# Two blocks of two gated attention layers: chunk 1 of layer 0 prepared ahead of the loop, input rows loaded chunk by chunk, Newton steps of eight layer norms on VectorE

## The reference

```
x = x + tanh(g_xattn[0]) * attention0(layernorm(x), context, context, prob, mask)
x = x + tanh(g_ffn[0])   * experts0(layernorm(x))
x = x + tanh(g_xattn[1]) * attention1(layernorm(x), context, context, mask1)
x = x + tanh(g_ffn[1])   * experts1(layernorm(x))
```

## Time and profile before

| what | us |
|---|---|
| median of 3 runs | 959.44 |
| lowest, highest | 957.41, 962.17 |
| the profiled execution, its own time | 961.64 |
| its span, first to last instruction | 959.8 |
| PE (TensorE) busy | 793.3 (83%) |
| DVE (VectorE) busy | 670.6 (70%) |
| ACT (ScalarE) busy | 608.5 (63%) |
| POOL (GpSimd) busy | 571.8 (60%) |

### The profile page before, as it was taken

The page is one execution under the profiler, slowest core; times in us unless marked ns, Lnnn a source line. Parts: engine busy times, 40 slices in busy tenths (PEclk is TensorE's granted clock), DMA queues, the critical chain, the costliest instruction groups (busy, mean ns, idle before and its releaser), DMA issues.

```text
span 959.8 us, 20423 instructions
## 1 busy us (share of the span) xinstructions
PE 793.3 (83%) x6554; PEld 627.5 (65%) x6554; DVE 670.6 (70%) x1933; ACT 608.5 (63%) x2582; POOL 571.8 (60%) x872
## 2 busy tenths in 40 slices
PE   2268898988886399999876788788986889999996
PEld 1146666766664299998555556656765767888885
DVE  1246889999896534436688799998896575666664
ACT  1366888998982255444787678889996344444442
POOL 6364567888777500223477887574341767777775
PEclk9978999999996699999999889999998899999998
DMA  7929789536633742322537367454300000000000
GB/s 172 243 87 242 197 218 274 138 98 157 128 86 130 259 138 83 85 82 85 110 85 140 72 127 173 112 109 120 89 13 24 22 23 23 21 15 14 8 12 22
DMA packets 83699, 101.68 MB, mean 106 GB/s; under 512 B 8289, under 2 KB 69926, under 8 KB 82665
## 3 DMA queue, kind: packets, MB, share of 16 engines
q1 hardware_dynamic: 79496, 92.13, 37.4%
q0 software_dynamic: 4096, 8.25, 3.5%
HBM read 63.32 MB, written 45.99 MB: 114 GB/s over the span
## 4 chain that ended last, share of the span: by engine, by line
PE 41%; DVE 22%; ACT 14%; POOL 9%; issue 9%; DMA 5%; SPq 0%; POOLq 0%; ACTq 0%; DVEq 0%
ACT exp L805 10%; PE psum L654 7%; PE psum L691 5%; PE psum L693 5%; PE psum L692 5%; DVE shift L986 5%; DVE exp_T L996 2%; PE psum L542 2%; PE psum L529 2%; PE psum L642 2%; DVE ln_stats L968 2%; PE psum L643 2%; PE psum L644 2%; DVE exp_T L998 2%; PE psum L707 1%
## 5 line engine op out<-in xcount | busy, mean ns | idle before, releaser
L805 ACT ACTIVATE exp<-psum,shift 128x120 f32<-128x120 f32 x1024 | 364.8, 427 | 92.9 <-DVE shift L986 92.5
L805 ACT ACTIVATION_READ_ACCUMULATOR exp<-psum,shift 128x1 f32 x1024 | 269.8, 273 | 0.0
L986 DVE TENSOR_REDUCE shift<-psum 128x4 f32<-128x480 f32 x256 | 164.9, 646 | 55.4 <-PE psum L520 54.8
L529 PE MATMUL psum<-ident,exp 128*120 128x128 f32 x1024 | 164.5, 285 | 35.1 <-DVE exp_T L998 22.0
L1569 POOL TENSOR_TENSOR q_operand<-q_operand 128x512 f32<-128x512 f32 x96 | 125.9, 1311 | 70.3 <-DVE q_operand L1345 66.1
L1345 DVE SCALAR_TENSOR_TENSOR q_operand<-psum,comb,q_operand 128x256 f32<-128x256 f32 x256 | 111.7, 479 | 79.9 <-ACT q_operand L933 79.9
L529 PEld LDWEIGHTS psum<-ident,exp 128*120 128x120 f32 x1024 | 120.4, 143 | 53.9 <-DVE exp_T L998 26.5
L933 ACT ACTIVATE q_operand<-psum 128x512 f32<-128x512 f32 x128 | 76.4, 598 | 122.3 <-PE psum L693 122.2
L1499 POOL DMA_INDIRECT got_rows<-scratch_y,slot_get x64 | 66.9, 1046 | 121.9 <-DMA scratch_y<-y_rows 104.5
L517 PE MATMUL psum<-neg_rows,const_bf 128*128 128x480 bf16 x256 | 98.7, 386 | 48.4 <-ACT exp L805 27.5
L691 PE MATMUL psum<-w_T_high,xn_T_high 128*128 128x512 f32 x256 | 108.8, 425 | 9.5 <-DVE w_T_low L1311 7.3
(11 more groups left out here) (164 smaller groups left out, 1557.5 us busy)
## 6 DMA issues: line engine op xcount, KB each, us to landing
k_operand<-scratch_k SPq DMA_DIRECT2D x32, 360.0 KB, 6.3
q_operand<-scratch_q SPq DMA_DIRECT2D x30, 384.0 KB, 6.1
scratch_q<-parts SPq DMA_DIRECT2D x15, 384.0 KB
scratch_k<-parts SPq DMA_DIRECT2D x14, 360.0 KB, 5.2
scratch_xe<-in_zero_rows SPq DMA_DIRECT2D x8, 512.0 KB, 12.6
scratch_y<-in_zero_rows SPq DMA_DIRECT2D x8, 512.0 KB, 6.9
scratch_q<-parts SPq DMA_DIRECT2D x15, 256.0 KB
scratch_k<-parts SPq DMA_DIRECT2D x14, 240.0 KB, 5.3
```

The costliest lines, as they stand in the source:

```text
L529: ins = pe.transpose(ps[0:S2, T_BANKS[G % 2], u * S:(u + 1) * S], atts[l].expS[:, G % RING_E, u, :], ident[:, :])
L805: ins = act.activation(atts[l].expS[:, G % RING_E, u, :], ps[:, S_BANKS[G % 3], u * S2:(u + 1) * S2], ACT.Exp, bias=atts[l].shift[:, i % 2 ...
L986: dve.tensor_reduce(atts[l].shift[:, i % 2, 4 * r:4 * r + 4], ps[:, S_BANKS[G % 3], 0:4 * S2].rearrange("p (h k) -> p h k", h=4), AX_X, AL ...
```

## The change

Four things are done.

1. **READY = 2.** Chunk 1 of layer 0 is prepared ahead of the loop, behind chunk 0, on all engines; looped() leaves it out of the loop. Chunks 0 and 1 are there normalised and split by VectorE, no longer by GpSimd. SyncE fetches chunk 0's k before it stores chunk 0's q, and clears only the first q buffer before that. Chunk 2 starts at slot 2 and chunk 3 at 10.
2. **load_rows by chunk.** Rows and context of chunk 2 are loaded ahead of the loop, those of chunk c from 3 on in slot 16 c - 46, with three semaphores in turn.
3. **Newton steps.** For eight layer norms (NEWTON_ON_DVE) GpSimd stops after pow, and VectorE does three operations (roots) in the slot of the powers. VectorE's normalise_rows then subtracts the mean and multiplies by the root, so that the product of both isn't needed.
4. **Slots.** Key splits behind layer 0 move from slots 2 and 5 to 5 and 8; the gathers of layer 1's chunks 5, 6 and 7 start at slot 30, 45 and 60, not 29, 37 and 52.

```diff
+NEWTON_ON_DVE = [(0, 0), (0, 1), (0, NCH), (0, NCH + 1), (0, NCH + 2), (0, NCH + 3), (1, NCH - 2), (1, NCH - 1)]
...
+def newton_on_dve(who, n):
...
+    return (who, n) in NEWTON_ON_DVE
...
 def start_slot(l, P):
-    return ({1: 0, 2: 5, 3: 14} if l == 0 else {1: 0, 2: 0, 3: 0}).get(P, 16 * P - 38)
+    return ({1: 0, 2: 2} if l == 0 else {1: 0, 2: 0, 3: 0}).get(P, 16 * P - 38)
...
+READY = 2
...
+def looped(l, P):
...
+    return l == 1 or P >= READY
...
 def prep_at(l, P):
-    return ({1: NEAR, 2: MID} if l == 0 else {1: NEAR1, 2: MID1, 3: FAR1, 4: FAR2}).get(P, FAR)
+    return ({2: MID} if l == 0 else {1: NEAR1, 2: MID1, 3: FAR1, 4: FAR2}).get(P, FAR)
...
 def bring_slot(i):
-    return {8: 0, 9: 7, 10: 9, 11: 11}[i] if c == 2 else {3: 13, 4: 21, 5: 29, 6: 37, 7: 52}[c] + 2 * b
+    return {8: 0, 9: 7, 10: 9, 11: 11}[i] if c == 2 else {3: 13, 4: 21, 5: 30, 6: 45, 7: 60}[c] + 2 * b
...
 def add_y_slot(i):
...
-SPLIT_KEYS_AT = {2: (0, 1), 5: (2,), 19: (3, 4, 5)}
+SPLIT_KEYS_AT = {5: (0, 1), 8: (2,), 19: (3, 4, 5)}
...
-    ld_first, ld_w, ld_rows = sem("ld_first"), sem("ld_w"), sems("ld_rows", 2)
+    ld_first, ld_w, ld_rows = sem("ld_first"), sem("ld_w"), sems("ld_rows", 3)
...
-            on.wait_ge(ld_rows[min(c, 2) - 1], 32)
+            on.wait_ge(ld_rows[c % 3], 32 * ((c - 1) // 3 + 1))
...
         def attention(l):
-                project_k(0)
-                turn_rows(0, 0)
-                project_q(0)
+                for C in range(READY):
+                    project_k(C)
+                    turn_rows(0, C)
+                    project_q(C)
...
         def attention(l):
-                take_projected(1, 0)
-                part0(1, 0)
-                take_turned(0, 0)
-                make_gates()
-                take_projected(0, 0)
-                part0(0, 0)
+                for C in range(READY):
+                    take_projected(1, C)
+                    part0(1, C)
+                    take_turned(0, C)
+                    take_projected(0, C)
+                    part0(0, C)
+                    if C == 0:
+                        make_gates()
...
+        def roots(who, n, h=0):
...
+            p = CB // 2 if h else CB
+            r_s, m_v = rs[:, who, :, 0:p], mv[:, who, 0:p, :]
+            power, rstd, m = (h_pow, h_rstd, 0) if h else (ln_pow[who], ln_rstd[who], n)
+            y, t_, r, v = (r_s[:, j, :] for j in (0, 1, 2, 4))
+            on.wait_ge(power, 2 * m + 2)
+            dve.tensor_tensor(t_, y, y, ALU.mult).then_inc(rstd, 1)
+            on.wait_ge(rstd, 6 * m + 1)
+            dve.scalar_tensor_tensor(t_, v, -0.5, t_, ALU.mult, ALU.mult).then_inc(rstd, 1)
+            on.wait_ge(rstd, 6 * m + 2)
+            dve.scalar_tensor_tensor(r, t_, 1.5, y, ALU.add, ALU.mult).then_inc(rstd, 4)
...
         def normalise_rows(who, n, c, h=0):
...
-                dve.tensor_scalar(xn[:, ln_slot(who, n), b, :], x[:, c * CB + b, :], rs[:, who, 2, b:b + 1], rs[:, who, 3, b:b + 1], ALU.mult, ALU.add).then_inc(ln_norm[who], 1)
+                dve.tensor_scalar(xn[:, ln_slot(who, n), b, :], x[:, c * CB + b, :], mv[:, who, b, 0:1], rs[:, who, 2, b:b + 1], ALU.subtract, ALU.mult).then_inc(ln_norm[who], 1)
...
         def slots(n):
...
+        def split(k, C):
+            left0(k, C)
+            part1(k, C)
+            left1(k, C)
...
         def split_keys(m):
...
+                    if o == at["power"]:
+                        roots(0, C)
...
+                if l == 0 and j >= ON_DVE and o == post_at(l, j)["power"]:
+                    roots(1, j)
...
+                    roots(0, NCH)
...
+                    roots(0, HALVED, 1)
...
+        roots(0, 0)
+        normalise_rows(0, 0, 0)
+        split(1, 0)
+        stat_rows(0, 1, 0, 1)
+        split(0, 0)
+        roots(0, 1)
+        normalise_rows(0, 1, 1)
+        split(1, 1)
...
+        split(0, 1)
...
+            if newton_on_dve(who, n):
+                return
...
         def behind(l, s):
...
+        powers(0, 0)
+        pool.memset(vx[:], 0.0).then_inc(spread0, 1)
+        powers(0, 1)
...
-        pool.memset(vx[:], 0.0).then_inc(spread0, 1)
-        left0(1, 0)
-        part1(1, 0)
-        powers(0, 0)
-        left1(1, 0)
-        normalise_rows(0, 0, 0)
...
-        left0(0, 0)
-        part1(0, 0)
-        left1(0, 0)
-        add_bias(0)
+        for C in range(READY):
+            add_bias(C)
...
     def sync_program(sp):
-        def load_rows(k, c0, c1):
-            sp.dma_start(x[:, c0 * CB:c1 * CB, :], t["x"][:, c0 * CB:c1 * CB, :]).then_inc(ld_rows[k], 16)
-            sp.dma_start(ctxT[:, c0 * CK:c1 * CK], t["ctxT"][:, c0 * CK:c1 * CK]).then_inc(ld_rows[k], 16)
...
-        def clear_spares(rings):
-            for r in range(rings):
+        def load_rows(c):
+            if c > 3:
+                wait_rows(on, c - 3)
+            sp.dma_start(x[:, c * CB:(c + 1) * CB, :], t["x"][:, c * CB:(c + 1) * CB, :]).then_inc(ld_rows[c % 3], 16)
+            sp.dma_start(ctxT[:, c * CK:(c + 1) * CK], t["ctxT"][:, c * CK:(c + 1) * CK]).then_inc(ld_rows[c % 3], 16)
...
+        def clear_spares(first, end):
+            for r in range(first, end):
...
-            on.wait_ge(spare_in, 32 * (RING if C <= NCH else RING + SPOILT))
+            on.wait_ge(spare_in, 32 * (1 if C == 0 else RING if C <= NCH else RING + SPOILT))
...
-            if l == 0 and s == 0:
-                load_rows(1, 2, NCH)
+            for c in range(READY + 1, NCH):
+                if l == 0 and s == 16 * c - 46:
+                    load_rows(c)
...
-                clear_spares(SPOILT)
+                clear_spares(0, SPOILT)
...
-        load_rows(0, 1, 2)
-        clear_spares(RING)
+        clear_spares(0, 1)
+        load_rows(1)
...
+        fetch_k(0)
...
-        fetch_k(0)
...
+        load_rows(2)
+        clear_spares(1, RING)
+        for p in range(3):
+            parts_out(1, 1, p)
+        for p in range(3):
+            parts_out(0, 1, p)
+        fetch_k(1)
+        fetch_q(1)
```

More of the change, by code:

```diff
@@ L582, in behind @@
                 o, at = s - start_slot(l, P), prep_at(l, P)
+                if not looped(l, P):
+                    continue
                 if o == at["k_project"] and l == 0:
```

## The result

| | median us | lowest to highest |
|---|---|---|
| kernel before (6 runs) | 961.77 | 957.41 to 962.37 |
| changed kernel (6 runs) | 951.60 | 949.78 to 952.58 |

The ratio is 0.9906, with a 95% interval of 0.9879 to 0.9933: faster by 9.0 us on 959.4 (the two medians are 10.2 apart). The forecast was 943, a gain of 16. The range held the result, and the direction was right; the size was not. The profiled execution took 951.59, its span is 949.8 and its mean granted clock 0.943. VectorE is busy for 686.9 us where it was 670.6, GpSimd for 545.9 where it was 571.8.

What follows compares the result with a forecast made beforehand. VectorE's row maxima pace attention, with time loose ahead of the loop, in chunk 0 and at layer 1's start. -14.8 + 2.7 - 1.6 - 2.4 + 0 = -16.1 gives 945.5 profiled, 943 on the median; range 932 to 955.

Steps and rivals of the forecast that it cites:

- The front (-14.8): Layer 0's chunk 0: first score at 33.4, not 38.5; slot 16 at 67.5 instead of 82.3, -14.8 us.
- Rival (a): Chunk 0: mask is all of it, landing past 60, slot 16 at 79; 955, no change; chance 0.08.
- (c): Freer front: k stored by 15, mask by 45, gathers pay 4; 933 us; chance 0.2.
- VectorE's splits beside the clearing (0 to +0.5): New front: VectorE splits while GpSimd clears memory, off the path; slowing from shared SBUF costs 0 to +0.5 us.
- Layer 0's end (+2.7 and -1.6): Chunk 6: VectorE stands 4.1 for pow, +2.7; chunk 7: earlier normalising, three key splits before logits, -1.6.
- Layer 1 (-2.4, and 0 for the gathers): Layer 1: Newton steps on VectorE bring -2.4 us net; later gathers for chunks 5 to 7 cost 0.
- Net +1.0 - 3.4 = -2.4: Layer 1, slots 6, 15, 24: VectorE's waits net +1.0; GpSimd, back to back, twice 1.7 earlier, -3.4.
- Half hidden behind ScalarE: Layer 1, slot 6: half of VectorE's first 1.9 us (pow wait plus Newton operations) is hidden behind ScalarE.
- given back out of the 3.65: Layer 1, slot 15: VectorE's second 1.9 us comes back out of its 3.65 wait for a gather at 529.5.
- The later gathers: I take 0, ends -4 and +4: Layer 1, chunks 5 to 7: gathers leave the crowded third chunk for the two after; 0, ends -4 and +4.
- the sign that would refute it: Forecast is wrong if first score comes after 38, GpSimd doesn't stand at the mask, or a layer 1 chunk grows.
- rival (b): VectorE's wait for pow in the loop: 4.1 + 0.5 at each of four hand-overs, 18 us; 971; chance 0.07.

Runs made afterwards that it cites:

- the mask's run: Changed kernel with chunk 1's mask asked for right behind chunk 0's q fetch, not in slot 0 of the loop; ratio 0.9877 to the kernel before.
- its run: Changed kernel with VectorE's Newton operations moved to the slot of the normalising, in layer 1's loop and layer 0's chunks 6 and 7; ratio 0.9835, 947.0 us.
- first run: Changed kernel with Newton steps of layer 1's chunks 1 (second half), 2 and 3 back on GpSimd; ratio 0.9874, 951.4 us.
- the three runs with another front: Changed kernel with chunk 1's mask asked for early, GpSimd's clearing of the second k operand late, or both; ratios 0.9877, 0.9939, 0.9891.

## Where the prediction was right, and where it was wrong

**The front (-14.8), right: -14.2 by slot 32.** The steps: k fetch 17.86 (18.7 forecast), q fetch 26.27 (27.5), first score on TensorE 33.34 (33.4), mask asked for at 42.99 (41), mask operation 52.4 (50), v_spread 55.98 (53.7), slot 16 at 71.3 (67.5; the forecast's own terms, 53.7 and seven slots of 1.9, give 67.0). The first score is met by two errors that cancel: both fetches were issued 0.8 to 1.2 early, and from the q fetch to the score it took 7.1 and not 5.8. At slot 16 the lead is 11.0 and not 14.8. The missing 3.2 came in chunk 1, which took 27.2 where the forecast kept 30.4. They lie in its first two slots, which took 3.23 and 2.34 us in the kernel before and 1.16 each here. There the kernel before had a granted clock of 0.50, its lower level, and the changed kernel 1.00 (columns PE, PEld, DVE, ACT, POOL, clock, DMA, GB/s):

```profile
82.80:86.22 3.42, 3.42 (x11) 1.69 (x9) 1.45 (x3) 2.32 (x10) 1.57 (x4) 0.50 0.97 350
```

So the sum is right partly by luck. The mechanism (mask behind all of SyncE's front, GpSimd standing at it, v_spread behind) is shown by the mask's run. Rival (a), the mask past 60, fell: the mask landed at 52.3. So did (c), which had it at 45 and 4 us from the gathers.

**VectorE's splits beside the clearing (0 to +0.5), wrong in size and without effect.** The forecast took 0.41 for a cast; that of q took 3.17 beside the clearing. It cost nothing, since q's stores waited behind k's fetch anyway.

**Layer 0's end (+2.7 and -1.6).** VectorE stood 4.14 (4.1 forecast) and normalised chunk 6 at 278.04. Row 289.65 of before less the 14.4 of the shift is 275.3: +2.8. Chunk 7's logits came at 298.39, before 313.00 - 14.4 = 298.6: -0.2, forecast +1.1. What the wait cost shows in its run: without it layer 1 starts 3.2 earlier.

**Layer 1 (-2.4, and 0 for the gathers): this is the step that failed.** It measured +4.4 where -2.4 was forecast, from two terms.
- "Net +1.0 - 3.4 = -2.4". Two of the three waits were sized rightly (1.50 and 1.49 measured, 1.4 forecast); the third, forecast as a replacement of 1.86, was 2.78. What went wrong is what was set against them. "Half hidden behind ScalarE" and "given back out of the 3.65": the changed kernel is 2.3 behind its shift at slot 7, 4.3 at slot 16, 8.9 at slot 25, so by then each wait had arrived in full and more, with maxima and exp_T queued behind it. Without the wait the first chunk ends 8.7 earlier against the start of the layer (first run), and 6.9 with the steps late. A part was given back, as forecast: 3.2 us at slot 32, where the kernel before stands 3.65 for its gather, and more up to slot 67, where 1.2 is left (2.1 to 2.9 in the three runs with another front). And the -3.4 for a GpSimd that is 1.7 earlier twice was no gain on the path: with the steps late and no wait, layer 1 wasn't shorter for having them on VectorE.
- "The later gathers: I take 0, ends -4 and +4". I priced where they leave (additions of 1.93 beside GpSimd's work) and not where they arrive. A gather takes 3.0 us to land in the median and up to 7.3 here, GpSimd was itself 7.5 us behind the slots (slot 67's gather ran at 604.1, that slot's maximum at 596.6), and the addition stands in slot 72. The last gather was issued at 604.13 and its rows were added at 611.46. From slot 67 to 73 the lead falls from 13.2 to 8.0; 1.9 come back by the end.

With both undone layer 1 is 6.4 shorter (one profile of each) and the ratio falls from 0.9906 to 0.984, with intervals that don't meet. How the 6.4 divides between the two stays open. The forecast named the sign that would refute it, a chunk of layer 1 that grows, and the first and fifth grew by 4.3 and 2.5. Its slower rival (b) named the right mechanism, VectorE's wait for pow in the loop; the price of 4.6 each was right once, at slot 124, and was 1.5 to 2.8 elsewhere.

**Sum:** -14.3 at the start of layer 1, +4.4 in it: -9.9, where the spans differ by 10.0.

## What to carry to other kernels

On an engine that works in order, put an instruction that needs another engine's result in the slot in which the result is consumed, not in that in which its input is ready; three small operations moved two or three slots later took away a wait of 4.1 us at the end of layer 0, and layer 1 began 3.2 us earlier. When gathers are moved later, count backwards from the addition: the landing at its worst, plus how far the issuing engine runs behind the slots. And when a gain early in a stretch doesn't arrive at its end, follow the lead slot by slot to the place where it goes: here one slot, 72, took 5 us. Whatever is issued in the front belongs in the queue by who waits for it first: one mask asked for 16 us earlier put the first maximum of chunk 1 6.7 us earlier.

## What the runs showed of the hardware

**A cast on VectorE stands still while GpSimd clears memory, a subtraction doesn't.** The timeline of the run with the clearing late, start and length:

```profile
24.73 6.54 POOL L1442 MEMSET k_operand<- 128x3840 uint32 x2
...
27.18 0.69 DVE L1181 TENSOR_TENSOR full<-full,parts 128x512 f32<-128x512 f32 x1 [4.97 <-ACT parts L797]
27.91 3.63 DVE L1190 CAST parts<-full 128x512 bf16<-128x512 f32 x1
31.58 0.69 DVE L1199 TENSOR_TENSOR parts<-full,parts 128x512 bf16<-128x512 f32 x1
```

The subtraction, inside the clearing, took its usual 0.69. The cast, 0.43 elsewhere, took 3.63 and ended at 31.54, 0.27 after the clearing; the one at 17.24 in the changed kernel ended 0.28 after its clearing. The Trainium skill (SBUF — State Buffer, Who interferes with whom) has it so: a VectorE instruction in a performance mode that uses both ports, as casts can be, and a GpSimd instruction exclude each other for their whole length, while one with two SBUF inputs contends only with a GpSimd instruction that reads SBUF. Both halves of that rule agree with these rows. The forecast weighed the second half alone.

**Indirect gathers**: 1.05 us of GpSimd each, 3.0 to land in the median and 7.3 at most, in the stretch from 560 to 612 us.

**The clock.** In layer 1's second chunk the granted clock was 0.77 in the changed kernel and 0.91 in the kernel before. It was 0.86 to 0.91 in four runs with layer 1's Newton steps on GpSimd, 0.81 to 0.82 in four with them on VectorE late, and 0.87 and 0.93 in two more of the latter. A part of the loss there may be the clock; no run separates it.

**The best kernel here** has three edits on the changed one: mask early, Newton steps late, gathers as before. It took 938.5 us (936.5 to 938.7) beside 960.9 for the kernel before: 22 us faster, where the change gave 9. With layer 1's Newton steps on GpSimd it is as fast (938.75).
